# A mixture-of-experts stage: x loaded in runs of 32 channels and turned blockwise by VectorE, result transfers spread over chunks

## The reference

```python
t = t + _L1_ffn_ref(_ln_t(t), router_w, w1, w2, w3)     # t: 8192 tokens x 64 channels, in float32
logits = flat @ router_w.T                               # 8 experts
topk_probs, topk_idx = top_k(softmax(logits), 2)         # two experts for each token
h = silu(flat @ w1[e].T) * (flat @ w3[e].T)              # 682 hidden channels
out = sum over the two chosen e of gate * (h @ w2[e].T)
```

## Time and profile before

| | |
|---|---|
| median of 3 runs | 988.93 us (986.78 to 991.55) |
| profiled execution | 986.66 us, span 984.9 us, granted clock 0.929 |
| TensorE, VectorE, ScalarE, GpSimd busy | 86%, 61%, 48%, 42% |
| DMA | 57.22 MB, mean 58 GB/s |

### The profile page before, as it was taken

One profiled execution on the slowest core, in us unless ns is written; L12 is line 12 of the kernel. 1 busy time (PEld: TensorE's weight loads), 2 busy tenths in 40 slices (PEclk: granted clock), 3 DMA queues, 4 the chain that ended last, 5 costly groups with the idle time before them and its releaser, 6 DMA issues.

```text
span 984.9 us, 24041 instructions
## 1 busy us (share of the span) xinstructions
PE 847.8 (86%) x8576; PEld 518.0 (53%) x8576; DVE 603.6 (61%) x1386; ACT 476.8 (48%) x933; POOL 412.0 (42%) x524
## 2 busy tenths in 40 slices
PE   4774799999999689969989778789999999999940
PEld 4444587777778556648777633223333333333530
DVE  1352587877878456745797855568565565655634
ACT  1042476666666434534554345445555555555520
POOL 0000345455454211100355556656666754444470
PEclk9885799999999789999989979989999999999985
DMA  7226200000000398000000030212031221111108
GB/s 192 57 63 121 51 9 11 10 9 11 8 11 3 119 339 255 2 3 2 16 18 21 22 74 23 58 41 54 25 76 44 57 50 38 45 38 45 42 3 256
DMA packets 103437, 57.22 MB, mean 58 GB/s; under 512 B 68261, under 2 KB 97793, under 8 KB 103360
## 3 DMA queue, kind: packets, MB, share of 16 engines
q1 hardware_dynamic: 89920, 46.61, 18.1%
q0 software_dynamic: 9088, 8.55, 2.7%
q10 hardware_dynamic: 4352, 1.05, 0.5%
HBM read 26.02 MB, written 28.97 MB: 56 GB/s over the span
## 4 chain that ended last, share of the span: by engine, by line
PE 33%; DMA 6%; POOL 5%; issue 4%; DVE 4%; ACT 2%; SPq 0%; ACTq 0%; POOLq 0%; DVEq 0%
PE bank L1350 18%; PE bank L1360 9%; DMA slot_x<-rows,slots 5%; POOL slot_x L1226 3%; PE bank L1336 2%; POOL chosen_out L1234 2%; PE bank L1369 2%; DVE norm_T L1755 1%; DMA ex_x<-slot_x 1%; PE bank L1283 1%; ACT norm_T L1465 1%; DVE residual L1772 1%; PE bank L1256 1%; DVE norm_T L1770 1%; DMA norm_T<-chosen_out 0%
## 5 line engine op out<-in xcount | busy, mean ns | idle before, releaser
L1755 DVE TENSOR_TENSOR norm_T<-norm_T,bank 114x512 f32<-114x512 f32 (+7 forms) x234 | 143.1, 636 | 150.7 <-ACT norm_T L1465 147.2
L1350 PE MATMUL bank<-ex_xt,ex_w 64*114 64x512 f32 (+7 forms) x936 | 214.9, 583 | 17.0 <-DVE norm_T L1755 13.5
L1234 POOL DMA_INDIRECT chosen_out<-ex_out,ex_id x156 | 155.8, 999 | 135.2 <-DVE ex_out L1707 74.3
L1465 ACT ACTIVATE norm_T<-bank 114x512 f32<-114x512 f32 (+7 forms) x234 | 129.7, 558 | 82.6 <-PE bank L1350 81.8
L1226 POOL DMA_INDIRECT slot_x<-rows,slots x128 | 123.8, 968 | 108.8 <-issue 63.8
L1350 PEld LDWEIGHTS bank<-ex_xt,ex_w 64*114 64x114 f32 x936 | 76.7, 177 | 106.4 <-issue 86.2
L462 POOL TENSOR_TENSOR probs<-shifted,win_rden 128x512 f32<-128x512 f32 x64 | 66.7, 1043 | 104.1 <-DVE win_rden L656 97.5
L1360 PE MATMUL bank<-norm_T,ex_w 114*64 114x512 f32 (+7 forms) x468 | 102.7, 574 | 0.3 <-ACT ex_w L1452 0.3
L1360 PEld LDWEIGHTS bank<-norm_T,ex_w 114*64 114x64 f32 x468 | 30.4, 139 | 69.2 <-issue 52.0
L642 DVE TENSOR_REDUCE win_max<-ps_s 128x8 f32<-128x512 f32 x64 | 43.9, 686 | 36.5 <-PE ps_s L502 36.5
L1458 ACT ACTIVATE norm_T<-bank 128x512 f32<-128x512 f32 (+7 forms) x39 | 21.8, 559 | 80.7 <-PE bank L1360 80.7
(11 more groups left out here) (261 smaller groups left out, 1499.2 us busy)
## 6 DMA issues: line engine op xcount, KB each, us to landing
slot_x<-blank SPq DMA_DIRECT2D x1, 17028.0 KB, 56.4
ex_x<-slot_x SPq DMA_DIRECT2D x39, 132.0 KB, 2.7
ex_x<-slot_x SPq DMA_DIRECT2D x39, 128.0 KB, 2.7
norm_T<-chosen_out SPq DMA_DIRECT2D x8, 512.0 KB, 6.8
w_in<-in_L_ffn_w_dram SPq DMA_DIRECT2D x24, 168.0 KB
chosen_out<-ex_out,ex_id POOLq DMA_INDIRECT x156, 2.2
wlocal_in<-in_L_conv_w_local_dram SPq DMA_DIRECT2D x2, 1152.0 KB, 7.3
norm_T<-in_x_dram SPq DMA_DIRECT2D x4, 512.0 KB, 8.9
```

The lines of the kernel that those rows point to most:

```text
L1234: eng.indirect_dma_start(s.chosen_out[:, :], bass.IndirectOffsetOnAxis(ex_id[k % OUTS][:, j:j + 1].bitcast(U32), 0), out[k % OUTS][:, j, : ...
L1350: eng.matmul(ps[b][0:HCHUNK, 0:width(k)], w13[par][halves(i), c * HCHUNK:(c + 1) * HCHUNK], xt[par][halves(i), 0:width(k)], start=True, st ...
L1465: eng.activation(act[c % DEEP][:, 0:width(k)], ps_1[c % DEEP][0:HCHUNK, 0:width(k)], ACT.Silu).then_inc(act_n, 1)
L1755: eng.tensor_tensor(h[par][:, c, 0:width(k)], act[c % DEEP][:, 0:width(k)], ps_3[c % deep3(k)][0:HCHUNK, 0:width(k)], ALU.mult).then_inc(h ...
```

## The change

x is loaded so that VectorE can turn it in blocks of 32x32. Partition band t (32 partitions, four bands) gets, from 16 blocks of 32 slots, 32 channels each: bands 0 and 2 channels 0 to 31, bands 1 and 3 channels 32 to 63. Gate and row number come in a fifth transfer to a tensor of their own, and only the used part of a narrow tile is loaded. `turn_in` moves from TensorE (behind the product) to VectorE (behind chunk 3), writes `xt` itself, and `across` goes. `turn_out` no longer waits for `ext_n`, since bank 0 is its own now. Slot r*depth+p lies at partition p. In `scatter` the second, third and fourth transfer wait for chunks 1, 2 and 3 of tile k+2 on VectorE, and each transfer names only the first `depth(k)` partitions.

```diff
-        x = [tmp(f"ex_x{i}", [P, R, C + ROW]) for i in range(4)]
+        x = [tmp(f"ex_x{i}", [P, SLOT]) for i in range(4)]
+        gate_id = [tmp(f"ex_gate_id{i}", [P, R, 2]) for i in range(4)]
-        slot_x = s.slot_x[:, :].rearrange("(k p r) c -> k p r c", p=P, r=R)
+        slot_x = s.slot_x[:, :].rearrange("(k n) c -> k n c", n=SLOT)
+        LOADS = 5
...
                     wait(eng, gate_n, k - 3)
-                    wait(eng, turned_n, k - 3)
+                    wait(eng, ext_n, k - 3)
                     tile = eng.value_load(table[t][0:1, k:k + 1], min_val=0, max_val=BLANK)
-                    src = slot_x[bass.ds(tile, 1)].rearrange("o p r c -> (o p) r c")
-                    eng.dma_start(x[k % 4][:, :, C:C + ROW], src).then_inc(x_in[k % 4], 16)
-                    eng.dma_start(x[k % 4][:, :, 0:C], src[:, :, 0:C]).then_inc(x_in[k % 4], 16)
+                    src = slot_x[bass.ds(tile, 1), 0:width(k), :]
+                    for band in range(4):
+                        lane = band % 2 * B32
+                        eng.dma_start(x[k % 4][band * B32:(band + 1) * B32, 0:width(k)].rearrange("t (b c) -> t b c", c=B32),
+                                      src[:, :, lane:lane + B32].rearrange("o (b t) c -> (o t) b c", t=B32)).then_inc(x_in[k % 4], 16)
+                    eng.dma_start(gate_id[k % 4][0:depth(k), :, :], src[:, :, C:C + 2].rearrange("o (r p) c -> (o p) r c", p=depth(k)),
+                                  allow_slow_non_contiguous=True).then_inc(x_in[k % 4], 16)
...
                     for j in range(R):
-                        eng.indirect_dma_start(s.chosen_out[:, :], bass.IndirectOffsetOnAxis(ex_id[k % OUTS][:, j:j + 1].bitcast(U32), 0),
-                                               out[k % OUTS][:, j, :], None, ...)
+                        if j > 0 and k + 2 < FTILES:
+                            eng.wait_ge(h_n, HCHUNKS * (k + 2) + j + 1)
+                        eng.indirect_dma_start(s.chosen_out[:, :], bass.IndirectOffsetOnAxis(ex_id[k % OUTS][0:depth(k), j:j + 1].bitcast(U32), 0),
+                                               out[k % OUTS][0:depth(k), j, :], None, ...)
...
-                def turn_in(k, buf, quarter):                    # TensorE, called behind product(k - 1)
-                    eng.wait_ge(x_in[buf], 32 * (quarter + 1))
-                    wait(eng, both_n, k - 2)
-                    for r in range(R):
-                        last = eng.transpose(ps_t[:, r * depth(k):(r + 1) * depth(k)], x[buf][0:depth(k), r, 0:2 * C], ...)
-                    last.then_inc(turned_n, 1)
...
-                    eng.wait_ge(ext_n, k + 3 if sym(k) else min(k + 3, FTILES))     # in turn_out
...
-                def across(k, par):                              # ScalarE
-                    eng.wait_ge(turned_n, k + 1)
-                    eng.activation(xt[par][:, 0:width(k)], ps_t[:, 0:width(k)], ACT.Copy).then_inc(ext_n, 1)
...
+                def turn_in(k, par, buf, quarter):               # VectorE
+                    eng.wait_ge(x_in[buf], 16 * LOADS * (quarter + 1))
+                    wait(eng, h3_n, HCHUNKS * (k - 1))
+                    eng.transpose(xt[par][:, 0:width(k)], x[buf][:, 0:width(k)]).then_inc(ext_n, 1)
...
+                        if c == 3 and before_last(k):
+                            turn_in(k + 1, 1 - par, (buf + 1) % 4, quarter + (buf + 1) // 4)
```

More of the change, by code:

```diff
@@ L998 @@
 ROW = C + 2
+B32 = 32
 RING = 6
@@ L1086, in dispatch_and_experts @@
         x_in = [sem(f"ex_x_in{i}") for i in range(4)]
-        gate_n, turned_n, ext_n, w13_n, w2_n, h1_n, h3_n, act_n, h_n, y_n, yc_n, eo_n, both_n, oc_n = (
-            sem(f"ex_{n}") for n in ("gate", "x", "xt", "w13", "w2", "h1", "h3", "act", "h", "y", "y_copied", "o", "o_halves", "o_copied"))
+        gate_n, ext_n, w13_n, w2_n, h1_n, h3_n, act_n, h_n, y_n, yc_n, eo_n, both_n, oc_n = (
+            sem(f"ex_{n}") for n in ("gate", "xt", "w13", "w2", "h1", "h3", "act", "h", "y", "y_copied", "o", "o_halves", "o_copied"))
         added = [sem(f"ex_added{i}") for i in range(OUTS)]
-        slot_x = s.slot_x[:, :].rearrange("(k p r) c -> k p r c", p=P, r=R)
+        slot_x = s.slot_x[:, :].rearrange("(k n) c -> k n c", n=SLOT)
+        LOADS = 5
         LAST = FTILES - 1
@@ L1233, in scatter @@
                     for j in range(R):
-                        eng.indirect_dma_start(s.chosen_out[:, :], bass.IndirectOffsetOnAxis(ex_id[k % OUTS][:, j:j + 1].bitcast(U32), 0),
-                                               out[k % OUTS][:, j, :], None, bounds_check=2 * TOK - 1, oob_is_err=False).then_inc(added[k % OUTS], 16)
+                        if j > 0 and k + 2 < FTILES:
+                            eng.wait_ge(h_n, HCHUNKS * (k + 2) + j + 1)
+                        eng.indirect_dma_start(s.chosen_out[:, :], bass.IndirectOffsetOnAxis(ex_id[k % OUTS][0:depth(k), j:j + 1].bitcast(U32), 0),
+                                               out[k % OUTS][0:depth(k), j, :], None, bounds_check=2 * TOK - 1, oob_is_err=False).then_inc(added[k % OUTS], 16)
                 eng.wait_ge(s.blank_n, 16)
@@ L1330, in _ @@
                         turn(chunk(g, 2))
-                def turn_in(k, buf, quarter):
-                    eng.wait_ge(x_in[buf], 32 * (quarter + 1))
-                    wait(eng, both_n, k - 2)
-                    for r in range(R):
-                        last = eng.transpose(ps_t[:, r * depth(k):(r + 1) * depth(k)], x[buf][0:depth(k), r, 0:2 * C], s.ident[0:depth(k), 0:depth(k)])
-                    last.then_inc(turned_n, 1)
                 def hidden(k, par, c):
@@ L1372, in body @@
                 def body(k, ring, eights):
-                    par, buf, quarter = ring % 2, ring % 4, 2 * eights + ring // 4
+                    par = ring % 2
                     for c in range(HCHUNKS):
@@ L1697, in keep @@
                         eng.wait_ge(added[ring], adds(eights))
-                    eng.wait_ge(x_in[buf], 32 * (quarter + 1))
-                    eng.tensor_copy(ex_gate[ring][:, :], x[buf][:, :, 2 * C])
-                    eng.tensor_copy(ex_id[ring][:, :], x[buf][:, :, 2 * C + 1]).then_inc(gate_n, 1)
+                    eng.wait_ge(x_in[buf], 16 * LOADS * (quarter + 1))
+                    eng.tensor_copy(ex_gate[ring][0:depth(k), :], gate_id[buf][0:depth(k), :, 0])
+                    eng.tensor_copy(ex_id[ring][0:depth(k), :], gate_id[buf][0:depth(k), :, 1]).then_inc(gate_n, 1)
+                def turn_in(k, par, buf, quarter):
+                    eng.wait_ge(x_in[buf], 16 * LOADS * (quarter + 1))
+                    wait(eng, h3_n, HCHUNKS * (k - 1))
+                    eng.transpose(xt[par][:, 0:width(k)], x[buf][:, 0:width(k)]).then_inc(ext_n, 1)
                 def result(k, ring):
@@ L1765, in _ @@
                 weights(0, 0)
+                turn_in(0, 0, 0, 0)
                 run(eng, body, tab_n)
```

6 lines of the change are left out of this document (removed).

## The result

The changed kernel takes 970.65 us (median of 4 runs, 969.74 to 972.41) against 987.86 us (984.74 to 991.55) of the kernel before on the same chip: ratio 0.9824, 95% interval 0.9801 to 0.9847, or 17.4 us. The forecast was 8.8 us. The profiled execution has a span of 969.5 us.

What follows compares the result with a forecast made beforehand. TensorE, 86% busy, was taken as the bound, GpSimd at the end. +2.1 at tile 13, +1.6 for the clock, -11.0 and -1.5 for turn-ins gave -8.8 us: forecast 980, own range 976 to 985, overall 968 to 992.

Steps and rivals of the forecast that it cites:

- The turn-in on TensorE: Four transposes a tile on TensorE's path: removing them saves 0.58 us a full tile, 1.5 us over tiles 33 to 36.
- The block transpose: VectorE, behind chunk 3: 0.71 us a full tile, ready 0.2 us before TensorE's next chunk 0, costing nothing.
- the saving of tiles 1 to 13 is lost whole, and tile 13 starts 2.1 us later than before: Waits between result transfers delay GpSimd's sends and so loads 5 and 13; tile 13 starts at 725.3 against 723.16.
- The load: Five transfers, 2640 packets at 20.4 ns, landing 5.3 us after first issue: hidden in the full stretch, 2.0 us where gated.
- The stall before tile 13: TensorE stands some 5 us before tile 13, then runs at the lower clock, adding 1.6 us.
- Wrong if load 13 is issued before 716: Sign against the forecast, which had load 13 issued near 718 (715.13 in the kernel before).
- Short transfers: GpSimd's result transfers of narrow tiles, 80 down to 16 rows: gain 0 taken, between 0 and about 9 us.
- Rival B: Short scatters at the end are cheap: 7 us more gain, -16 down to -18, 973 to 971; chance 0.14.
- Rival A: Load 13 is not late, so tiles 8 to 13 keep 3.5 us: -16, 973; chance 0.12.

Runs made afterwards that it cites:

- idle transposes: Changed kernel with four transposes of the identity put back on TensorE for every tile, their output read by nothing: ratio 0.9971 to the kernel before.
- before, new order of the sends: Kernel before, with the router's sends in two pieces of 8 per chunk, each waiting for the piece before it to have landed: ratio 0.9930.
- changed, again: The changed kernel run once more with no edit, beside the kernel before: ratio 0.9849, span 965.9 us.

## Why the prediction was wrong in size

The direction and most mechanisms held; the gain was twice the forecast.

- **The turn-in on TensorE**: 0.58 us a tile predicted, 9.46 to 8.88 measured, and 13 us come back with the idle transposes. Right.
- **The block transpose**: 0.71 us predicted, 0.705 measured (mean of the 32 full ones), cover 0.2 predicted, 0.3 by the rows and by the kernel that turns twice. Right, and by a thin margin. The Trainium skill ("VectorE: DVE Perf Modes", The three transpose paths) has 311 ns for 128x128 in 16 bit. My estimate from it, four times that or 1.24 us, does not hold for float32 in one instruction of 512 columns: 0.705.
- **The step that failed: "the saving of tiles 1 to 13 is lost whole, and tile 13 starts 2.1 us later than before".** It starts 4.7 us earlier, so 6.8 us of error. I took chunk 3 of tile 2 and chunk 3 of tile 5 from the profile of before, and in the changed kernel's they come 3.8 and 7.4 us earlier, counted from the first load. With the late times the waits cost 5 us, as the kernel that has only the waits shows; with the early ones they cost nothing in one execution and 0.8 us at scatter(0) in the other. Of the 3.8, 1.2 are there at chunk 0 of tile 0, which comes 5.52 us after the first load and not 6.75. The missing turn-ins behind it are not the rest: with those of tiles 1 to 38 put back, chunk 3 of tile 2 still comes at 39.23. What goes with it is the clock in the first tiles:

  | profiled execution of | product of tile 0, us | chunk 3 of tile 2 | scatter(0), start to next send |
  |---|---|---|---|
  | before | 3.40 | 42.62 | 5.3 (no waits) |
  | only the waits | 3.70 | 42.96 | 10.0 |
  | changed, without the waits | 3.65 | 41.99 | 5.2 (no waits) |
  | changed, transpose twice | 3.77 | 43.14 | 10.6 |
  | before, new order of the sends | 2.80 | 40.56 | 5.2 (no waits) |
  | changed | 2.80 | 38.80 | 5.2 |
  | changed, again | 2.79 | 39.01 | 6.0 |
  | changed, idle turn-ins | 2.80 | 39.23 | 5.2 |

  Where the product of tile 0 takes 2.80 us the granted clock over it is 1.00; in the first four rows it is 0.73 to 0.82. The old kernel and the changed one each stand on both sides, in one or two profiles apiece, so what decides it is open, and that the waits found chunk 3 done was partly luck. Tile 5 is another matter. On TensorE its chunk 3 follows its chunk 0 by 7.8 us after and by 12.9 before, where 3.6 us of waits for VectorE and a product of 4.66 us instead of 2.80 lie between, besides the turn-in.

  Of the 6.8, 3.2 are there when the sends go on behind scatter(3). Another 1.9 come between there and load 13, where I had the old 66.1 us and it took 64.25: before, GpSimd waits 3.74 and 3.28 us for two of its five landings there, after, none takes over 2.15. Why is open; it is 64.3 in the kernel that has only the waits and 64.65 in the changed one without them. The last 1.8 lie between load 13 and chunk 0 of tile 13 (below).
- **The load**: I took 20.4 ns a packet and a landing 5.3 us after the first issue, with 1.0 added for waits and denser loads. It was 12.3 ns in the mean, and tile 13's chunk 0 comes 5.40 us after the issue where I had 7.2: the turn starts 4.44 us after it, 1.0 sooner than my 5.3 and 0.1 for the signal, and the 1.0 for waits (0.04 us each) and denser loads did not come, since the gap between transfers is 0.30 with a wait that finds its chunk done and without one. The Trainium skill ("DMA: Bandwidth & Descriptors", Why small descriptors are slow) has some 3 cycles of overhead for each packet. My estimate by it, about 13 ns for 128 B, lies close to the traces: 12.3 with the short ones in, 13.8 for each one added when the loads are doubled. I had left it out of my sum. The load costs only at the gates, as predicted (2.1 to 2.3 us at each when it is doubled).
- **The stall before tile 13**: about 5 us predicted, 4.69 measured, with 2.2 us for the lower clock behind it (twelve matmuls 4.99 us against 2.83, granted clock 0.55), predicted 1.6. Its size was luck: load 13 was not late, TensorE was early (done with tile 12 at 149.2 us after the first load, where chunk 0 of tile 13 began at 158.57 before). "Wrong if load 13 is issued before 716" was the sign to look at, and 148.47 against 150.54 says so.
- **Short transfers**: 0 predicted, 2.0 to 2.1 measured alone; the term was mis-sized since no row of before had fewer than 128 rows. Rival B (973 to 971) named the time, 970.65 and 971.88, but by luck: it had 7 us for the short transfers, which gave 2.
- Rival A (load 13 not late) had the mechanism, and 973. I gave it 0.12. Its argument against, 0.7 us of cover, asked only about load 13 and not when the chunks would come that it hung on. That its sum came so near is partly luck too: it has neither the 2.2 us of the lower clock nor the 2.0 of the short transfers, which cancel.

The sum as measured: -4.7 before tile 13, -11.0 -1.5 for the turn-ins behind it, +2.2 for the clock, -2.0 for the short transfers: -17.0, against -17.7 in the traces. The -11.0 and -1.5 are the predicted terms; the idle turn-ins bear them out together. The 0.7 is within what executions differ by: the second trace of the changed kernel is 20.1 us shorter than before from the first load to the end, and the two ratios say 17.4 and 14.9.

## What to carry to other kernels

A new wait is to be judged against the time at which its releaser comes in the changed kernel: move the releaser's own chain first, and only then ask who waits. Give that time a range as well: here chunk 3 of tile 2 came anywhere from 38.8 to 43.1 us, by the clock of the first tiles, and the waits held GpSimd for nothing to 5.4 us by it. Saving work on the bounding engine ahead of a gate turns into a stall at the gate unless what opens the gate moves too; here a few lines in the order of the sends were worth 10 us more. A term without any row in the trace, like the 16-row transfers, deserves a value between its ends, not the end at which it is nothing.

## What the runs showed of the hardware

- An indirect transfer issued by GpSimd of 256 floats a row takes 0.98 us for 128 rows, 0.91 for 64, 0.88 for 48 and 0.84 for 16: seven eighths of the rows fewer save 0.14 us.
- A load's packets (2048 of 128 B, 512 of 8 B, 80 others) took 12.3 ns of a DMA engine in the mean, and each one added by doubling the 128 B ones 13.8; packets of 256 and 264 B took 20.4 ns; twice as many of the 128 B ones, at a DMA share of 0.49, slowed neither TensorE nor VectorE.
- A fifth transfer of 512 runs of 8 B was issued in 0.39 us, quicker than the 128 B ones, four of which take 1.94 (0.49 each); at both gates its landing is the one named as releasing VectorE.
- A wait of 0.31 us for the first matmul of a tile cost 0.53 us of the tile (9.41 us against 8.88).
- Behind an idle time of 4.69 us TensorE ran twelve matmuls in 4.99 us at granted clock 0.55, behind one of 1.37 us (transpose twice) in 2.83 us at 1.00.
